# Layer 0's front of a two-layer AdaLN kernel: inverse roots by ln and exp on ScalarE, other orders on the engines, a shorter routing

## The chip, the cores and the metric

The kernel runs on one NeuronCore of a Trainium2 chip. The metric is device time in microseconds (us) of the whole program, one launch; lower is better. Engines: PE is TensorE, DVE is VectorE, ACT is ScalarE, POOL is GpSimd, SP is SyncE, which here only issues DMAs. Each engine works through its own queue in order, and queues wait for each other by semaphores.

## The reference, cut to what matters

A batch of 8 sequences of 512 tokens with 128 channels goes through two layers, each an attention part and a mixture-of-experts part with modulated layernorms. The change is in layer 0, up to the table that says which tokens each expert takes:

```python
mod = (_silu(L0_c) @ L0_wmod).reshape(8, 6, 1, -1); sa, ca, ga, sb, cb, gb = ...
h = _layernorm(x) * (1 + ca) + sa
u = rmsnorm(h) * norm_w                       # x * rsqrt(mean(x*x) + 1e-6)
# a first-order recurrence over the 512 tokens for 64 states, then y = states @ C + D
x = x + ga * y
h = _layernorm(x) * (1 + cb) + sb
wg_n = wg / max(norm(wg), 1e-4)
idx = argmax(softmax((h @ w_red) @ wg_n.T))   # one of 8 experts for each token
# each token goes through its expert only
```

A layernorm needs 1/sqrt(variance + eps) for each token, the rmsnorm 1/sqrt(mean square + eps).

## The kernel before, in words

The 4096 tokens lie as 32 tiles of 128 tokens. A tile holds 64 tokens of each of two sequences (a pair), so there are 4 pairs `bp` of 8 tiles each (1024 columns). Everything in the front is written by hand, pair by pair, as five straight lists of instructions, one for each engine; the order in a list is the order on that engine. Stage `k` is 0 for the first layernorm, 1 for the second.

For each pair: `measure(k, bp)` (DVE: 8 bn_stats, L1088, and five small operations, L1093 to L1097, that give sum and variance); `root` (ACT, sqrt of 8 columns, L741); `rates` (DVE, reciprocal L1102 and a product L1103); the normalising, half a pair on ACT (`norm`, L748) and half on POOL (`norm_too`, L506); `turn_rows` (PE transposes, L1725); for k=0 `first_hT` and `squares` (ACT, L771 and L781), `up_and_squares` (PE, L1735 and L1737: projections and sums of squares), `rms_and_up` (ACT, L788 sqrt and L789 copy), `invert_rms` (DVE reciprocal of 512 columns, L1107), `scale_up` (DVE, L1112), `scan` (DVE, the recurrence, L1118), `read_states` (PE, L1747), `add_y0` (DVE, L1123, which adds the result to x in place and needs POOL's `add_d`, L499, to have been there first). For k=1: `second_hT` (ACT, L795), `first_logits` (PE, 8 products of 8 columns each for a pair, L1764), and `back_rows` (PE, L1757) with `rows_back` (ACT, L803), which turn the rows back so that SP can store them.

After the last logits (semaphore `lg_mm`) DVE does the routing: maximum and one-hot choice (L1210 to L1218), two products on PE that count tokens ahead and in all (L1806, L1807), sums over tiles (L1223 to L1237), slot numbers, one-hot matrices for slots and tiles (L1248 to L1250, L1205), and 32 products on PE (L1820) that give the list of tokens by slot. PE's part of layer 1's modulation (L1717, L1704) lies between the counting and these. `tokens_set` then lets POOL gather rows (L558), and the expert loop follows. From the loop on, the program is the same in both kernels.

Pools and buffers don't decide an order here: each buffer has its place, and the waits are written out. Two pairs share each buffer in turn (`bp % 2`).

## Time and profile before

| | us |
|---|---|
| median of 3 runs | 815.23 (805.23 to 819.42) |
| the profiled execution, its time | 815.39 |
| its span, within that | 813.7 |
| x's first pair measured, start | 8.15 |
| last logits done, routing begins on DVE | 76.15 |
| token list done (end of L1256) | 94.49 |
| first product of the expert loop | 104.80 |

Over the span PE is busy 709.0 us (87%), DVE 640.1 (79%), POOL 579.5 (71%), ACT 476.6 (59%). A span begins with the first instruction and ends with the last; the time of the execution is 1.7 us longer. Line numbers are those of the kernel before. The granted clock is the share of TensorE's full clock: 1.00 is 2.4 GHz, 0.50 is 1.2 GHz. The trace counts an fp32 product as two records.

### The profile page before, as it was taken

The page shows a single profiled execution, that of the slowest core. Times are in us where ns is not written, and L with a number is a line of the kernel's source. Part 1 is how long each engine was busy: PE and PEld are TensorE (multiplying, and loading weights), DVE is VectorE, ACT ScalarE, POOL GpSimd, SP SyncE. Part 2 cuts the span into 40 slices and gives each one's busy share as a digit, 9 for nine tenths or more (in the row PEclk, how much of TensorE's full clock was granted, in tenths as well). Part 3 has the DMA queues.
Part 4 walks back from the last instruction along what each step waited for, and adds up shares of the span by engine and source line. Part 5 has one row for each costly group of instructions (what it writes and reads, how often), then busy time and mean ns, then how long its engine had stood idle before and what let it go on. Part 6 is the DMA issues. An engine that isn't in the chain of part 4 may idle for free.

```text
span 813.7 us, 34138 instructions
## 1 busy us (share of the span) xinstructions
PE 709.0 (87%) x14873; PEld 650.1 (80%) x14874; DVE 640.1 (79%) x1048; ACT 476.6 (59%) x757; POOL 579.5 (71%) x431
## 2 busy tenths in 40 slices
PE   4568778767899999999999999999999998776997
PEld 3357577767788899998899898888999888676897
DVE  6994745379678989999899998999899998866215
ACT  5735234328746756786676677667667764548510
POOL 4811277267789889989889988888788788732750
PEclk8685599999899999999999999999999999985999
DMA  8401324310520000000000000000000000061128
GB/s 336 178 27 53 118 75 96 73 37 9 153 71 13 8 6 6 8 10 6 6 6 8 19 3 3 18 3 3 4 16 4 3 17 17 3 231 56 50 61 293
DMA packets 33583, 42.89 MB, mean 53 GB/s; under 512 B 4000, under 2 KB 25648, under 8 KB 32928
## 3 DMA queue, kind: packets, MB, share of 16 engines
q1 hardware_dynamic: 29856, 33.99, 12.2%
q0 software_dynamic: 3296, 6.76, 3.6%
q8 instruction: 117, 1.92, 1.0%
q14 instruction: 26, 0.21, 0.1%
q10 hardware_dynamic: 288, 0.01, 0.0%
HBM read 26.65 MB, written 14.09 MB: 50 GB/s over the span
## 4 chain that ended last, share of the span: by engine, by line
PE 68%; DVE 12%; issue 10%; POOL 4%; DMA 2%; ACT 2%; DVEq 1%; POOLq 0%; SPq 0%; ACTq 0%
PE psum L1900 18%; PE psum L1955 7%; PE psum L1933 6%; PE psum L2000 6%; PE psum L1991 4%; PE psum L1948 4%; PE psum L1962 4%; PE psum L1970 3%; PE psum L1838 3%; PE psum L1941 2%; PE psum L2258 1%; PE psum L1764 1%; PE psum L1848 1%; DVE small L1430 1%; POOL y_rows L713 1%
## 5 line engine op out<-in xcount | busy, mean ns | idle before, releaser
L1900 PE MATMUL psum<-hT,w_qkv 128*128 128x128 f32 x1408 | 175.7, 282 | 5.8 <-ACT hT L914 2.7
L1900 PEld LDWEIGHTS psum<-hT,w_qkv 128*128 128x128 f32 x1408 | 166.0, 196 | 9.4 <-ACT hT L914 2.8
L617 POOL TENSOR_TENSOR arena<-arena,small 128x1024 f32<-128x1024 f32 x56 | 106.1, 1916 | 40.3 <-DVE small L1449 40.2
L596 POOL TENSOR_TENSOR arena<-arena 128x1024 f32<-128x1024 f32 x56 | 106.8, 1907 | 14.1 <-ACT arena L957 13.1
L582 POOL TENSOR_TENSOR arena<-arena 128x1024 f32<-128x1024 f32 x56 | 106.7, 1905 | 0.1
L1442 DVE TENSOR_REDUCE small<-arena 128x16 f32<-128x1024 f32 x60 | 73.0, 1218 | 12.7 <-ACT arena L946 10.5
L621 POOL TENSOR_TENSOR arena<-arena 128x1024 f32<-128x1024 f32 x28 | 65.9, 2355 | 13.1 <-DVE arena L1469 13.1
L1430 DVE TENSOR_REDUCE small<-psum 128x16 f32<-128x1024 f32 x60 | 72.8, 1215 | 0.2 <-PE psum L2000 0.2
L1436 DVE TENSOR_TENSOR arena<-psum,small 128x1024 f32<-128x1024 f32 x60 | 70.4, 1214 | 0.1
L926 ACT ACTIVATE arena<-psum 128x1024 f32<-128x1024 f32 x28 | 28.7, 1025 | 70.0 <-PE psum L1900 70.0
L558 POOL DMA_INDIRECT arena<-h_rows,route x39 | 39.7, 1018 | 39.2 <-issue 37.7
L2000 PE MATMUL psum<-arena 64*64 64x128 f32 x1792 | 61.0, 277 | 7.4 <-issue 4.4
L1955 PE MATMUL psum<-w_o,arena 128*128 128x128 f32 x512 | 65.5, 282 | 0.9 <-ACT arena L973 0.6
L946 ACT ACTIVATE arena<-arena 128x1024 f32<-128x1024 f32 x60 | 62.9, 1051 | 4.7 <-DVE arena L1436 4.5
L1933 PE MATMUL psum<-arena 64*128 64x64 f32 x1344 | 61.8, 230 | 3.7 <-issue 2.2
L1955 PEld LDWEIGHTS psum<-w_o,arena 128*128 128x128 f32 x512 | 60.5, 194 | 4.8 <-issue 3.4
L2000 PEld LDWEIGHTS psum<-arena 64*64 64x64 f32 x1792 | 51.2, 134 | 11.9 <-issue 10.0
L1933 PEld LDWEIGHTS psum<-arena 64*128 64x128 f32 x1344 | 49.5, 139 | 10.5 <-issue 2.8
L931 ACT ACTIVATE arena<-psum 128x1024 f32<-128x1024 f32 x28 | 28.7, 1026 | 35.2 <-PE psum L1933 35.2
L1461 DVE TENSOR_TENSOR arena<-arena,psum 128x1024 f32<-128x1024 f32 x28 | 34.0, 1216 | 17.5 <-PE psum L1991 17.4
L544 POOL DMA_INDIRECT arena<-o_rows,route x32 | 33.0, 1030 | 20.4 <-DMA o_rows<-arena 13.6
L859 ACT ACTIVATE arena<-psum,route 128x128 f32<-128x128 f32 x78 | 21.4, 380 | 43.8 <-PE psum L1838 43.8
(334 smaller groups left out, 1624.0 us busy)
## 6 DMA issues: line engine op xcount, KB each, us to landing
y_rows<-hT SPq DMA_DIRECT2D x8, 512.0 KB, 6.7
arena<-in_L_W_rows SPq DMA_DIRECT2D x2, 2048.0 KB, 10.6
arena<-y_rows SPq DMA_DIRECT2D x8, 512.0 KB, 8.0
o_rows<-arena SPq DMA_DIRECT2D x9, 256.0 KB
x_sb<-in_x_rows SPq DMA_DIRECT2D x4, 512.0 KB, 6.1
arena<-in_L_W_rows SPq DMA_DIRECT2D x2, 1024.0 KB, 9.7
arena<-in_W_in_rows SPq DMA_DIRECT2D x4, 512.0 KB, 14.9
arena<-in_W_out_rows SPq DMA_DIRECT2D x4, 512.0 KB, 9.4
```

Source lines behind the costliest of these rows:

```text
L582: pool.tensor_tensor(w4, w4, d4.unsqueeze(3).to_broadcast([P, 2, HP, D]), ALU.mult).then_inc(done, 1)
L596: pool.tensor_tensor(x3, x3, lr[:, tile_of(t) * 32 + k * H:tile_of(t) * 32 + k * H + H].unsqueeze(2).to_broadcast([P, H, D]), ALU.mult).th ...
L617: pool.tensor_tensor(z4, z4, r3.unsqueeze(3).to_broadcast([P, 8, 2, CH]), ALU.mult).then_inc(done, 1)
L621: pool.tensor_tensor(g_tok, g_tok, p_tok, ALU.mult).then_inc(g_done, 1)
L946: act.activation(z, z, ACT.Exp, scale=0.5).then_inc(z_exp, 1)
L1430: dve.tensor_reduce(z_max[:, 16 * jh:16 * jh + 16], h3(ps[2 + jh]), AX_X, ALU.max).then_inc(z_maxed, 1)
L1436: dve.tensor_tensor(h3(zs[t % 2][:, jh * 1024:(jh + 1) * 1024]), h3(ps[2 + jh]), z_max[:, 16 * jh:16 * jh + 16].unsqueeze(2).to_broadcast( ...
L1442: dve.tensor_reduce(z_sum[t % 2][:, 16 * jh:16 * jh + 16], h3(zs[t % 2][:, jh * 1024:(jh + 1) * 1024]), AX_X, ALU.add).then_inc(z_added, 1)
L1900: mm = pe.matmul(ps[bank][:, p * P:(p + 1) * P], w_qkv[:, j * HD + p * P:j * HD + (p + 1) * P], hT[:, at:at + P], start=True, stop=True)
L1933: mm = pe.transpose(out[:, col((r, 2), (n, HP))], of[half(r), at(n):at(n) + P], eye[half(r), :])
L1955: mm = pe.matmul(y_bank(t), oT_buffer(t)[:, n * P:(n + 1) * P], w_o[:, n * C:(n + 1) * C], start=(n == 0), stop=(n == HP - 1))
L2000: mm = pe.matmul(out, w_in[t % BP][half(r), col((be, 2), (p, HP))], x4[half(r), :, p, be, :], start=True, stop=True)
```

## The change

1. `root` and `rms_and_up` take ln instead of sqrt, and an exp with scale -0.5 follows on ACT, which gives the inverse root. The reciprocals on DVE (L1102, L1107 and one for the experts' norms) go. For the four pairs the exp of the rmsnorm is a new ACT step, `inverse_rms(bp)`. One table set holds both functions; it is loaded behind the third exp of the start. ACT's list has three table loads up to the expert loop instead of four: the one in front of the exp of the logits goes.
2. Other orders on ACT, DVE, POOL and PE. On DVE `measure(0, 1)` stands ahead of `rates(0, 0)`; on ACT `root(0, 1)` stands ahead of `norm(0, 0)`, and `norm(0, 1)` directly behind it.
3. `keep_warm` products, whose results nobody reads: 10 at the start, 9 behind the gates, 4 ahead of `up_and_squares(0)`, 4 ahead of `first_logits(2)`.
4. Routing: the logits are read from PSUM, the one-hot matrix is written as bf16 at once, eight scans of 32 columns become one of 256, a subtraction goes into the counting matrix (`before_less` holds -1 and 0), tiles are counted by a shift instead of compare and reduce, and the right-hand sides of the 32 products are made in four parts, so that PE may start after the first.

SP's list is the same. The diff, cut to its core:

```diff
+            chain.link(pool.tensor_scalar(before_less, before_less, -1.0, None, ALU.add))
+            chain.link(pool.memset(later_tiles, 1.0))
+            chain.link(pool.memset(later_tiles.rearrange("p (e t) -> p e t", t=T)[:, :, 0], 0.0))
...
             norm_too(0, 0)
+            norm_too(0, 1)
             pool.wait_ge(a0_gates, 2)
             pool.wait_ge(a0_in, 16 * 3)
             chain.link(pool.tensor_tensor(d_gated.rearrange("p (b c) -> p b c", c=C), over_pairs(mod0, 0), over_tiles(d_bc, BP), ALU.mult))
-            norm_too(0, 1)
             add_d(0)
+            add_d(1)
             norm_too(0, 2)
-            add_d(1)
+            add_d(2)
             norm_too(0, 3)
-            add_d(2)
             add_d(3)
...
+            act.preload_act_table_set("natural_log_exp_and_others")
...
                 act.wait_ge(fr_var[k], bp + 1)
-                act.activation(rstd[:, a:b], var[:, a:b], ACT.Sqrt, bias=ln_eps, scale=1.0 / C).then_inc(fr_std[k], 1)
+                chain.link(act.activation(rstd[:, a:b], var[:, a:b], ACT.Ln, bias=ln_eps, scale=1.0 / C))
+                act.activation(rstd[:, a:b], rstd[:, a:b], ACT.Exp, scale=-0.5).then_inc(fr_std[k], 1)
...
                 act.wait_ge(a0_up, bp + 1)
                 after(act, a0_scan, bp - 1)
-                act.activation(rms[bp % 2], ps[2][:, L:2 * L], ACT.Sqrt, bias=rms_eps, scale=1.0 / C).then_inc(a0_rms, 1)
+                act.activation(rms[bp % 2], ps[2][:, L:2 * L], ACT.Ln, bias=rms_eps, scale=1.0 / C).then_inc(a0_rms, 1)
                 act.activation(ups[bp % 2], ps[2][:, 0:L], ACT.Copy).then_inc(a0_rms, 1)
+
+            def inverse_rms(bp):
+                act.wait_ge(a0_rms, 2 * bp + 1)
+                act.activation(rms[bp % 2], rms[bp % 2], ACT.Exp, scale=-0.5).then_inc(a0_rec, 1)
...
             def rates(k, bp):
                 a, b = bp * NC, (bp + 1) * NC
                 dve.wait_ge(fr_std[k], bp + 1)
-                chain.link(dve.reciprocal(rstd[:, a:b], rstd[:, a:b]))
                 dve.scalar_tensor_tensor(sums[:, a:b], sums[:, a:b], -0.5, rstd[:, a:b], ALU.mult, ALU.mult).then_inc(fr_rates[k], 1)
-
-            def invert_rms(bp):
-                dve.wait_ge(a0_rms, 2 * bp + 1)
-                dve.reciprocal(rms[bp % 2], rms[bp % 2]).then_inc(a0_rec, 1)
...
             measure(0, 0)
+            measure(0, 1)
+            rates(0, 0)
             dve.wait_ge(mod_out, 1)
             plus = mod_cols[0].rearrange("c (k s b) -> c k s b", k=2, s=2)[:, :, 0, :]
             dve.tensor_scalar(plus, plus, 1.0, None, ALU.add).then_inc(cols_set, 1)
-            rates(0, 0)
-            measure(0, 1)
+            dve.wait_ge(mod_out, 2)
+            chain.link(dve.tensor_scalar(half_sign, ps[3], 0.0, 0.5, ALU.is_ge, ALU.subtract))
+            rates(0, 1)
+            dve.wait_ge(gw, 32)
+            chain.link(dve.tensor_tensor(wg_n[0:E, :], wg_s[0:E, :], wg_s[0:E, :], ALU.mult))
+            chain.link(dve.tensor_reduce(wg_t[0:E, 0:1], wg_n[0:E, :], AX_X, ALU.add))
...
             chain.link(dve.scalar_tensor_tensor(mod0[:, :], mod0[:, :], 0.5, half_sign, ALU.max, ALU.mult))
-            rates(0, 2)
             dve.sem_inc(a0_gates, 1)
             dve.tensor_tensor(c_gated.rearrange("p (b c) -> p b c", c=C), over_pairs(mod0, 0), over_tiles(cmat, BP), ALU.mult).then_inc(a0_gates, 1)
+            measure(0, 2)
             dve.wait_ge(gw, 34)
-            chain.link(dve.tensor_scalar(wg_t[0:E, 1:2], wg_n[0:E, 0:1], 1e-4, None, ALU.max))
-            chain.link(dve.reciprocal(wg_t[0:E, 2:3], wg_t[0:E, 1:2]))
             dve.tensor_scalar(wg_n[0:E, :], wg_s[0:E, :], wg_t[0:E, 2:3], None, ALU.mult).then_inc(gw, 1)
-            measure(0, 3)
+            rates(0, 2)
             dve.wait_ge(gw, 36)
             dve.tensor_copy(wg_t[0:16, :], ps[3][0:16, 0:E]).then_inc(gw, 1)
-            invert_rms(0)
-            rates(0, 3)
+            measure(0, 3)
+            dve.wait_ge(gw, 38)
+            dve.tensor_copy(w_gate, ps[3][:, 512:512 + E]).then_inc(gw, 1)
             scale_up(0)
             scan(0)
-            dve.wait_ge(gw, 38)
-            dve.tensor_copy(w_gate, ps[3][:, 512:512 + E]).then_inc(gw, 1)
-            invert_rms(1)
+            rates(0, 3)
             add_y0(0)
+            measure(1, 0)
             scale_up(1)
-            measure(1, 0)
             scan(1)
             rates(1, 0)
-            invert_rms(2)
             scale_up(2)
+            scan(2)
             add_y0(1)
-            invert_rms(3)
-            scan(2)
+            measure(1, 1)
             scale_up(3)
             scan(3)
...
-            dve.tensor_copy(logits, ps[2][:, L:L + T * E]).then_inc(lg_out, 1)
-            dve.wait_ge(lg_out, 1)
+            logits = ps[2][:, L:L + T * E]
             chain.link(dve.tensor_reduce(mx, te(logits), AX_X, ALU.max))
             chain.link(dve.tensor_tensor(te(shifted), te(logits), over_e(mx), ALU.subtract))
             chain.link(dve.scalar_tensor_tensor(te(pick), te(shifted), 0.0, over_t(first_w), ALU.is_equal, ALU.mult))
             dve.tensor_reduce(m2, te(pick), AX_X, ALU.max).then_inc(oh_done, 1)
             dve.wait_ge(oh_done, 1)
-            chain.link(dve.tensor_tensor(te(onehot), te(pick), over_e(m2), ALU.is_equal))
-            dve.tensor_copy(onehot_b, onehot).then_inc(rhs_ready, 1)
+            dve.tensor_tensor(te(onehot_b), te(pick), over_e(m2), ALU.is_equal).then_inc(rhs_ready, 1)
...
-            before_p, totals = ps[3][:, 0:256], ps[3][:, 512:768]
-            for e in range(E):
-                last = dve.tensor_tensor_scan(te(cum)[:, :, e], ones_f[:, 0:T], te(totals)[:, :, e], 0.0, ALU.mult, ALU.add)
-            chain.link(last)
-            chain.link(dve.tensor_tensor(rank, cum, totals, ALU.subtract))
-            chain.link(dve.tensor_tensor(rank, rank, before_p, ALU.add))
-
-            cnt = te(cum)[:, T - 1, :]
-            c3 = n_cmp[:, 0:E * T].rearrange("p (e t) -> p e t", t=T)
-            chain.link(dve.tensor_tensor(c3, cnt.unsqueeze(2).to_broadcast([P, E, T]), over_t(edges, E), ALU.is_gt))
-            chain.link(dve.tensor_reduce(n_tiles[:, 0:E], c3, AX_X, ALU.add))
+            by_e = lambda ap: ap.rearrange("p (e t) -> p e t", t=T)
+            not_before, totals = ps[3][:, 0:256], ps[3][:, 512:768]
+            chain.link(dve.tensor_tensor_scan(cum, later_tiles, totals, 0.0, ALU.mult, ALU.add))
+
+            cnt = by_e(cum)[:, :, T - 1]
+            dve.tensor_scalar(tile_i[:, 0:E], cnt, float(P - 1), None, ALU.add).then_inc(tiles_counted, 1)
+            chain.link(dve.tensor_tensor(rank, cum, not_before, ALU.add))
+            dve.wait_ge(tiles_counted, 1)
+            chain.link(dve.tensor_scalar(tile_i[:, 0:E], tile_i[:, 0:E], 7, None, ALU.arith_shift_right))
+            chain.link(dve.tensor_copy(n_tiles[:, 0:E], tile_i[:, 0:E]))
             chain.link(dve.tensor_tensor_scan(t_end[:, 0:E], ones_f[:, 0:E], n_tiles[:, 0:E], 0.0, ALU.mult, ALU.add))
             chain.link(dve.tensor_tensor(t_start[:, 0:E], t_end[:, 0:E], n_tiles[:, 0:E], ALU.subtract))
-            chain.link(dve.tensor_scalar(t_start[:, 0:E], t_start[:, 0:E], float(P), None, ALU.mult))
-            chain.link(dve.tensor_tensor(te(rank), te(rank), over_t(t_start[:, 0:E]), ALU.add))
-            chain.link(dve.tensor_tensor(rank, rank, onehot, ALU.mult))
-            chain.link(dve.tensor_reduce(slot_f, te(rank), AX_X, ALU.add))
+            chain.link(dve.scalar_tensor_tensor(by_e(rank), t_start[:, 0:E].unsqueeze(2).to_broadcast([P, E, T]), float(P), by_e(rank),
+                                                ALU.mult, ALU.add))
+            chain.link(dve.tensor_tensor(by_e(rank), by_e(rank), onehot_b.rearrange("p (t e) -> p e t", e=E), ALU.mult))
+            chain.link(dve.tensor_reduce(slot_f, rank.rearrange("p (e t) -> p t e", t=T), AX_X, ALU.add))
             chain.link(dve.tensor_copy(slot_i[:, 0:T], slot_f))
             chain.link(dve.tensor_scalar(tile_i, slot_i[:, 0:T], 7, None, ALU.arith_shift_right))
+            dve.tensor_copy(tile_b, tile_i)
             chain.link(dve.tensor_copy(tile_f, tile_i))
-            dve.tensor_copy(tile_b, tile_f)
...
             chain.link(dve.tensor_tensor(t4(tile_hot), slot_tiles, over_s(tile_b), ALU.is_equal))
-            dve.tensor_tensor(t4(t_rhs[:, 0:T * 40]), t4(tile_hot), over_s(tile_nb), ALU.mult)
-            dve.tensor_scalar(t_rhs[:, T * 40:T * 80], tile_hot, part_no, None, ALU.mult).then_inc(rhs_ready, 1)
             for i in range(T // 8):
+                here = slice(i * 320, (i + 1) * 320)
+                dve.tensor_tensor(t4(t_rhs[:, 0:T * 40])[:, i], t4(tile_hot)[:, i], over_s(tile_nb)[:, i], ALU.mult)
+                made = dve.tensor_scalar(t_rhs[:, T * 40:T * 80][:, here], tile_hot[:, here], part_no, None, ALU.mult)
+                if i == 0:
+                    made.then_inc(rhs_ready, 1)
                 slots_hot(r_hot, i)
...
+            pe.wait_ge(consts_made, 1)
+            keep_warm(10, ps[2][:, 0:P])
             columns(0)
             gate_rows()
-            pe.wait_ge(consts_made, 1)
+            keep_warm(9, ps[2][:, 0:P])
             turn_rows(0, 0, ps[0])
             pe.wait_ge(mod_out, 1)
-            pe.wait_ge(a0_gates, 1)
-            up_and_squares(0)
             turn_rows(0, 1, ps[1])
             pe.wait_ge(gw, 35)
             pe.transpose(ps[3][0:16, 0:E], wg_n[0:E, :], ident[0:E, 0:E]).then_inc(gw, 1)
-            turn_rows(0, 2, ps[0])
+            keep_warm(4, ps[2][:, 0:P])
+            pe.wait_ge(a0_gates, 1)
+            up_and_squares(0)
             pe.wait_ge(gw, 37)
             pe.matmul(ps[3][:, 512:512 + E], wred_t[0:16, :], wg_t[0:16, :], start=True, stop=True).then_inc(gw, 1)
+            turn_rows(0, 2, ps[0])
             up_and_squares(1)
             pe.wait_ge(gw, 39)
             pe.wait_ge(a0_gates, 3)
             read_states(0)
             turn_rows(0, 3, ps[1])
             up_and_squares(2)
+            read_states(1)
             up_and_squares(3)
             turn_rows(1, 0, ps[0])
-            read_states(1)
+            read_states(2)
             back_rows(0)
+            read_states(3)
+            turn_rows(1, 1, ps[0])
             pe.wait_ge(a0_rms, 8)
             first_logits(0)
-            read_states(2)
-            read_states(3)
-            turn_rows(1, 1, ps[0])
+            back_rows(1)
             first_logits(1)
             turn_rows(1, 2, ps[0])
-            back_rows(1)
             pe.wait_ge(a0_added, 4)
             turn_rows(1, 3, ps[3])
+            keep_warm(4, ps[2][:, 0:P])
             first_logits(2)
             first_logits(3).then_inc(lg_mm, 1)
             back_rows(2)
             back_rows(3)
 
             pe.wait_ge(rhs_ready, 1)
-            pe.matmul(ps[3][:, 0:T * E], before, onehot_b, start=True, stop=True)
-            pe.matmul(ps[3][:, 512:512 + T * E], all_ones, onehot_b, start=True, stop=True).then_inc(cnt_done, 1)
+            hot_by_e = onehot_b.rearrange("p (t e) -> p e t", e=E)
+            by_e = lambda ap: ap.rearrange("p (e t) -> p e t", t=T)
+            pe.matmul(by_e(ps[3][:, 0:T * E]), before_less, hot_by_e, start=True, stop=True)
+            pe.matmul(by_e(ps[3][:, 512:512 + T * E]), all_ones, hot_by_e, start=True, stop=True).then_inc(cnt_done, 1)
```

On DVE, from the last small copy ahead of the first pair's recurrence on. L1107 is the reciprocal of 512 columns, L1112 the scaling, L1118 the scan, L1123 the addition into x. Before:

```order
L1169 COPY arena<-psum 16x8
L1107 RECIPROCAL arena<-arena 128x512
L1102 RECIPROCAL small<-small 128x8
L1103 SCALAR_TENSOR_TENSOR small<-small 128x8
L1112 TENSOR_TENSOR arena<-arena 128x512
L1118 SCALAR_TENSOR_TENSOR arena<-arena 128x512
L1175 COPY arena<-psum 128x8
L1107 RECIPROCAL arena<-arena 128x512
L1123 TENSOR_TENSOR x_sb<-x_sb,psum 128x1024
```

Now, where L1122 is the scaling, L1128 the scan, L1133 the addition:

```order
L1179 COPY arena<-psum 128x8
L1122 TENSOR_TENSOR arena<-arena 128x512
L1128 SCALAR_TENSOR_TENSOR arena<-arena 128x512
L1117 SCALAR_TENSOR_TENSOR small<-small 128x8
L1133 TENSOR_TENSOR x_sb<-x_sb,psum 128x1024
L1103 BN_STATS arena<-x_sb 128x6 x8
```

The two long reciprocals and the wait of the second one are gone from between scan and addition; the third pair's are gone likewise.

On PE, the last third of the front, beginning with the second pair's `read_states`. L1747 is `read_states`, L1757 `back_rows`, L1764 `first_logits`, L1725 `turn_rows`. Before:

```order
L1747 MATMUL psum<-arena 64x128 x16
L1757 MATMUL psum<-ident,hT 128x64 x16
L1764 MATMUL psum<-arena,hT 128x8 x8
L1747 MATMUL psum<-arena 64x128 x32
L1725 MATMUL psum<-ident,arena 128x64 x16
L1764 MATMUL psum<-arena,hT 128x8 x8
L1725 MATMUL psum<-ident,arena 128x64 x16
L1757 MATMUL psum<-ident,hT 128x64 x16
L1725 MATMUL psum<-ident,arena 128x64 x16
L1764 MATMUL psum<-arena,hT 128x8 x16
```

Now, beginning with the third pair's; L1751 is `read_states`, L1761 `back_rows`, L1768 `first_logits`, L1729 `turn_rows`, L1699 the products that nobody reads:

```order
L1751 MATMUL psum<-arena 64x128 x16
L1761 MATMUL psum<-ident,hT 128x64 x16
L1751 MATMUL psum<-arena 64x128 x16
L1729 MATMUL psum<-ident,arena 128x64 x16
L1768 MATMUL psum<-arena,hT 128x8 x8
L1761 MATMUL psum<-ident,hT 128x64 x16
L1768 MATMUL psum<-arena,hT 128x8 x8
L1729 MATMUL psum<-ident,arena 128x64 x32
L1699 MATMUL psum<-ident 128x128 x4
L1768 MATMUL psum<-arena,hT 128x8 x16
```

The first pair's logits (8 products) have moved behind the last `read_states`, and four spare products stand ahead of the last sixteen logits.

On POOL, from the first `norm_too` on; L499 is `add_d`, L513 makes `d_gated`. Before:

```order
L506 TENSOR_SCALAR arena<-x_sb,small 128x128 x4
L513 TENSOR_TENSOR arena<-mod,arena 128x512
L506 TENSOR_SCALAR arena<-x_sb,small 128x128 x4
L499 TENSOR_TENSOR x_sb<-x_sb,arena 128x1024
L506 TENSOR_SCALAR arena<-x_sb,small 128x128 x4
L499 TENSOR_TENSOR x_sb<-x_sb,arena 128x1024
L506 TENSOR_SCALAR arena<-x_sb,small 128x128 x4
L499 TENSOR_TENSOR x_sb<-x_sb,arena 128x1024 x2
L506 TENSOR_SCALAR arena<-x_sb,small 128x128 x16
```

Now, where L508 is `norm_too`, L501 `add_d`, L516 `d_gated`:

```order
L508 TENSOR_SCALAR arena<-x_sb,small 128x128 x8
L516 TENSOR_TENSOR arena<-mod,arena 128x512
L501 TENSOR_TENSOR x_sb<-x_sb,arena 128x1024 x2
L508 TENSOR_SCALAR arena<-x_sb,small 128x128 x4
L501 TENSOR_TENSOR x_sb<-x_sb,arena 128x1024
L508 TENSOR_SCALAR arena<-x_sb,small 128x128 x4
L501 TENSOR_TENSOR x_sb<-x_sb,arena 128x1024
L508 TENSOR_SCALAR arena<-x_sb,small 128x128 x16
```

The second pair's normalising has moved ahead of `d_gated`, and the third pair's behind two of the additions to x.

## Rows read from the trace of the kernel before

**Rows 1.** The page's first line: the profiled execution.
```profile
span 813.7 us, 34138 instructions
```
**Rows 2.** Windows by stage: start:end, length; busy PE, PEld, DVE, ACT, POOL; clock; DMA share; GB/s.
```profile
8.15:33.05 24.90, 14.84 (x88) 9.07 (x88) 23.60 (x78) 18.07 (x37) 14.02 (x21) 0.66 0.86 345
33.05:53.42 20.37, 12.07 (x146) 8.21 (x144) 18.30 (x26) 11.95 (x20) 7.54 (x9) 0.92 0.10 28
53.42:76.15 22.73, 19.23 (x178) 18.16 (x180) 12.15 (x51) 10.74 (x22) 5.25 (x12) 0.65 0.08 24
76.15:94.49 18.34, 14.44 (x82) 9.80 (x82) 13.36 (x42) 8.86 (x13) 0.00 (x0) 0.59 0.28 87
```
**Rows 3.** Groups by line, first 96 us: busy, mean ns, idle before.
```profile
L1107 DVE RECIPROCAL arena<-arena 128x512 f32<-128x512 f32 x4 | 13.4, 3343 | 1.2 <-ACT arena L788 1.2
```
**Rows 4.** Chain of waits, up to the expert loop: start, us, what.
```profile
48.95 3.35 DVE arena L1107
...
69.16 6.96 PE psum L1764 x32
```
**Rows 5.** Timeline of the front: start, us, engine line operation [idle before].
```profile
11.44 1.64 DVE L1088 BATCH_NORM_STATS2 arena<-x_sb 128x6 f32<-128x128 f32 x8
...
15.68 1.45 ACT L781 ACTIVATE arena<-psum,small 128x512 f32<-128x512 f32 x2
...
19.30 0.18 ACT L815 ACTIVATE arena<-arena 8x1 f32<-8x1 f32 x1
...
23.04 0.57 ACT L789 ACTIVATE arena<-psum 128x512 f32<-128x512 f32 x1
...
31.69 1.36 DVE L1118 TENSOR_TENSOR_SCAN arena<-arena 128x512 f32<-128x512 f32 x1
...
41.75 0.30 ACT L741 ACTIVATE small<-small 128x8 f32<-128x8 f32 x1 [1.03 <-DVE small L1097]
```
**Rows 6.** Timeline, VectorE beside GpSimd.
```profile
24.19 2.41 DVE L1094 TENSOR_TENSOR arena<-arena 128x8 f32<-128x8 f32 x1
...
24.22 2.36 POOL L499 TENSOR_TENSOR x_sb<-x_sb,arena 128x1024 f32<-128x1024 f32 x1
...
31.16 3.02 POOL L506 TENSOR_SCALAR arena<-x_sb,small 128x128 f32<-128x128 f32 x4 [0.53 <-DVE small L1103]
```
**Rows 7.** Timeline, TensorE, in order of time.
```profile
45.80 1.96 PE L1747 MATMUL psum<-arena 64*64 64x128 f32 x32
...
48.34 1.95 PE L1764 MATMUL psum<-arena,hT 128*128 128x8 f32 x16
...
53.42 3.68 PE L1747 MATMUL psum<-arena 64*64 64x128 f32 x32 [3.14 <-DVE arena L1118]
...
58.80 1.96 PE L1747 MATMUL psum<-arena 64*64 64x128 f32 x32 [1.70 <-DVE x_sb L1123]
...
96.84 4.60 PE L1695 MATMUL psum<-ident 128*128 128x128 f32 x20 [3.08 <-DVE route L1267]
```
**Rows 8.** Windows of TensorE, 1 us each: busy (count), granted clock, DMA share, GB/s.
```profile
64.00:65.00 1.00, 1.00 (x7) 0.51 0.00 0
```
**Rows 9.** Chain of waits, routing.
```profile
78.37 1.12 PE psum L1757 x16
...
80.07 1.01 DVE arena L1223 x8
...
81.10 0.43 DVE arena L1225
...
82.47 0.43 DVE route L1231
...
86.74 0.83 DVE arena L1249
...
88.03 0.61 DVE arena L1205
...
88.77 5.00 PE psum L1820 x32
```

51 lines of the change are left out of this document (24 added, 27 removed).

## The prediction

> **What bounds the kernel now.** I read the windows by stage first. The front ends where the routing begins, at 76.15 us, the routing takes 18.34 us more, and the rest of the span of 813.7 us [rows 1] is the same program in both kernels. So all that can come or go lies in the first 94.49 us. Up to 53.42 us DVE is busy for 23.60 of 24.90 and 18.30 of 20.37 us, ACT for 18.07 and 11.95, PE for 14.84 and 12.07: DVE is full, the others wait. From 53.42 to 76.15 PE takes over with 19.23 of 22.73 us at a mean granted clock of 0.65 [rows 2]. The groups by line name DVE's largest item, four reciprocals of 512 columns, 3343 ns each, 13.4 us in all [rows 3]. The chain of waits keeps this from being simple: it passes through only one of the four, and then through 6.96 us of logits on PE [rows 4]. The other three ran beside waits of POOL, ACT and PE.
>
> **Up to the first scan.** The first pair starts later now: measure(0,1) costs 1.64 us of bn_stats [rows 5] and about 0.8 of small operations and stands ahead of rates(0,0), and norm(0,0) waits for root(0,1). From DVE's start at 8.15, two measures of 2.4 us give 13.0, the second root and rate 13.5, norm(0,0) and norm(0,1) 16.8, first_hT and squares, 1.45 us each [rows 5], and 0.4 for the two small roots, 20.1. Before, squares(0) ran from 15.68 to 17.13: 3.0 us late. What follows makes it good. On POOL norm_too(0,2) stands behind d_gated and two additions of 2.36 us [rows 6]: about 18.0 + 1.1 + 4.7 = 23.8, plus up to 2.0 where DVE holds it up, so turn_rows(0,2) comes at about 27.5. On ACT, squares(0) at 20.1, root(0,2), first_hT(1), norm(0,2), rms_and_up(0), squares(1) and inverse_rms(0) make 0.5 + 1.45 + 1.65 + 1.25 + 1.45 + 0.6 = 6.9, with 1 to 2 us of waits: 28.5. Scaling and scan (0.7 + 1.36 [rows 5]) would end at 30.6 unhindered; an addition on POOL of 2.36 can stand in front of them: 32.9. I take 31.5, against 33.05: **-1.5 us**, ends -2.5 and 0.
>
> **What the roots cost.** Sqrt of 8 columns was 0.30 us and a small activation without a bias 0.18 [rows 5]; ln then exp is 0.30 + 0.20, in place of 0.30 on ACT and 0.20 of reciprocal on DVE: nothing on the path, 0.2 us off DVE eight times. A 512-column copy took 0.57 us [rows 5]; I take that for the exp, in place of 3.34 on DVE: 2.8 us shorter each time it lies on the path. No trace shows ln; the bounds are the same rows, ±0.1 us each time.
>
> **From the first scan to the last read_states.** Before, this took from 33.05 to 60.76 [rows 7], 27.7 us. Three reciprocals go, 10.0, and 1.2 of waiting for their input [rows 3]. If DVE were the only bound read_states(3) would end at 60.8 - 1.5 - 11.2 = 48.1. It is not: ACT now has, behind inverse_rms(0) at 28.5, root, first_hT, norm, rms_and_up, squares, inverse (6.95 us), then first_hT, root, rms_and_up, inverse, squares, norm, rms_and_up, inverse (8.8), so the last inverse is at 44.3 without a wait and at 46.5 with two or three of a microsecond. Behind it stand scaling, scan, the third pair's addition (1.2) and 1.96 us of products [rows 7]: 46.5 + 0.7 + 1.4 + 1.2 + 2.0 = 51.8. I take **52**, ends 48 and 56: 8.8 us earlier than before.
>
> **PE's tail.** Before, from 60.76 to 76.11 PE did turn, logits(1), turn, back, turn and 16 tiles of logits. Now logits(0), which ran at 48.34 in a gap for 1.95 us [rows 7], lies in the tail, with four spare products. What each costs depends on the clock: 8 tiles of logits took 1.95 us at 2.4 GHz and 6.96 / 2 = 3.48 at 1.2; ten spare products took 4.60 at 1.2 [rows 4, 7], so four take 1.84, and half that at 2.4. The row of the windows at 64 us shows the clock at 0.51 [rows 8], 3.2 us behind the end of read_states(3), with only transposes and logits on PE between, and it stayed at 1.2 GHz through all later transposes and logits. I expect the same: turn 0.7, logits(0) 1.95, back 0.9, logits(1) 3.48, two turns 2.2, spare 1.84, logits(2, 3) 6.96 are 18.0, so 52 + 18.0 = **70.0**, against 76.15: **-6.1 us** for the front (ends -2 and -10). Of the 8.8 us that the head gains the tail gives back 2.7.
>
> **Routing.** Ahead of the counting products, the copy (0.46) and the cast (0.3) go from DVE, which I cost at nothing: these products stand behind back_rows(3) on PE, which ran to 79.49 [rows 9], 0.3 us after DVE had been ready, and that chain stays. Behind them: eight scans 1.01 become one of 256 columns, half of 1.36, say 0.65: -0.4. One subtraction, -0.45. Compare and reduce, 0.43 each, become three operations of 8 columns at 0.2: -0.3. One small product, -0.2, one cast, -0.1. Of the right-hand sides only a quarter stands ahead of PE's start: 0.83 + 0.46 becomes 0.40, -0.9; the four quarters are each shorter (1.0 us with their 0.61 of slots) than the 5.00 / 4 = 1.25 in which PE eats one [rows 9]. Together **-2.4 us**, ends -1.6 and -3.2 (a strided reading of the one-hot matrix by PE and DVE is new; a wider product cost no more than 0.4 here, and I bound it by 0.8). The modulation on PE gets 1.28 us shorter through the missing table load, so it still ends ahead of the slots.
>
> Sum: -6.1 - 2.4 = -8.5, so 815.4 - 8.5 = **807 us**. The profiled execution (815.39) and the median of the runs (815.23) differ by 0.2, so this is also the sum for the median.
>
> **The additions on POOL.** At 24.19 one DVE operation of 8 columns with two SBUF inputs took 2.41 us and ended with POOL's addition of 2.36 that began beside it (26.60 and 26.58) [rows 6]. The reciprocals have one input, and all four took 3.34 [rows 3], though additions ran beside some of them. Four normalisings on POOL took 3.02 us while DVE's scan of 1.36 lay in them [rows 5, 6], so it goes both ways. With the reciprocals gone, measure(0,3), scaling and scan now meet additions. My 31.5 holds one to two of these. The Trainium skill, SBUF — State Buffer, section "Who interferes with whom", says that the two engines take a shared port pair for a whole instruction when the DVE instruction has two SBUF inputs and GpSimd reads SBUF, and that the other blocks fully. The row agrees, once; by the rule all four additions can block, and the sum would be rival C's.
>
> **Rivals.**
> A. *Forecast*, clock falls behind the last read_states: 807, own range 802 to 812. Chance 0.5.
> B. *The clock stays.* The four spare products, denser work ahead of them or a shorter gap keep 2.4 GHz through the tail. Then the tail is 0.7 + 2 + 0.7 + 2 + 1.4 + 0.9 + 3.9 = 11.6, but second_hT(3) on ACT becomes the bound and adds 1 to 2: 52 + 13 = 65, and if it lasts, 1 us of the 5.00 of the token list: 807 - 5 - 1 = 801. For it: dense products bring the clock back, read_states(2) took 3.68 us and read_states(3) 1.96 [rows 7]. Against: ten spare products took 4.60 us, all of it at the pace of 1.2 GHz [rows 7], and here there are four. Chance 0.2.
> C. *POOL's additions block three times more*: 3 x 2.36 = 7.1 on DVE's path: 814. For it: no reciprocal covers them. Against: DVE has slack once ACT is the bound. Chance 0.13.
> D. *Slower: the reciprocals were hidden.* The chain of waits has only one of them, 3.35 us. If no more comes off the path, and the first pair's late start is carried to the end (3.0), and its exp (0.6) and the longer tail (3.48 + 1.84) are paid, the sum is -3.35 + 3.0 + 0.6 + 5.3 - 2.4 = +3.2: 818.5. It decides at the end of read_states(3): past 58 us it is this case. Against: DVE was busy for 0.9 of the time up to there. Chance 0.1.
> That an extra table load spoils the change is excluded: ACT's list has one load for all roots, ahead of the first, which waits for the variance (8.15 + 2.4 = 10.6).
>
> **Numbers.** What is left, 0.07, is scatter: the three runs before reach from -10.0 to +4.2 us around their median. The range of 796 to 816 takes in A, B and C with some of that scatter, and leaves out D and the low end. A measurement of this kernel tells about 2% from no change, 16.3 us, so faster means below 798.9: a third of B and a little scatter, 0.11. Slower means above 831.5: 0.02. Within: 0.87.
>
> **What would show it.** Right: scan(0) ends at 30 to 33 us, read_states(3) at 49 to 55, the last logits at 67 to 73 with a clock of 0.5, token list 15.9 us later. Wrong: squares or rates that wait in ACT's and DVE's lists for POOL and move read_states(3) past 56; logits at 1.0; counting products above 0.8 us; or an expert loop whose 708.9 us change by more than scatter, which I cost at nothing, since its program is the same.

## The result, and the profile after

The changed kernel takes 803.28 us (median of 20 runs, 797.19 to 810.97), the kernel before 810.41 in the same comparison (805.23 to 819.42): a ratio of 0.9907, 95% interval 0.9880 to 0.9933, so 7.1 us less. Its profiled execution has a span of 795.8 us, 17.9 us less than before. 10.7 us of that come from the expert loop onward (104.80 to 813.7 before, 97.55 to 795.8 after), where the program is the same. In the twelve experiments below this stretch took 695.6 to 705.1 us whatever the front, 698.1 in one with the old orders ("roots only"); so the 708.9 us of the kernel before are the long end of the scatter, and the forecast is judged in the front, by waypoints. The changed kernel was profiled a second time (first of the experiments), which shows how far each waypoint holds.

| end of | before | forecast | after | after, second |
|---|---|---|---|---|
| scan(0) | 33.05 | 31.5 | 34.73 | 34.10 |
| read_states(3) | 60.76 | 52.0 | 56.19 | 54.25 |
| last logits | 76.11 | 70.0 | 70.18 | 71.14 |
| token list | 94.49 | 85.9 | 87.20 | 88.19 |

In the kernel before TensorE ended the logits at 76.11, and the routing's first operation on DVE began at 76.15, where its stage is cut.

The page's first line and the windows by stage (start:end, length; busy PE, PEld, DVE, ACT, POOL; clock; DMA share; GB/s), which answer to [rows 1, 2]; line numbers are those of the changed kernel from here on:

```profile
span 795.8 us, 34239 instructions
```
```profile
7.82:34.73 26.91, 16.02 (x111) 11.59 (x113) 20.34 (x72) 17.68 (x39) 16.66 (x24) 0.76 0.82 326
34.73:56.19 21.46, 16.32 (x198) 11.30 (x196) 16.45 (x52) 17.45 (x36) 8.95 (x13) 0.90 0.10 27
56.19:70.18 13.99, 13.99 (x139) 13.67 (x140) 4.13 (x17) 8.83 (x17) 3.50 (x8) 0.74 0.12 35
70.18:87.20 17.02, 13.76 (x82) 9.43 (x82) 12.28 (x38) 7.58 (x12) 0.00 (x0) 0.70 0.33 96
```

DVE is no longer full in the first two stages (20.3 of 26.9 and 16.5 of 21.5 us). The stage up to the first scan got longer all the same, 26.91 us instead of 24.90. The timeline of DVE, ACT and POOL (start, duration, both us; in brackets the idle time before and what ended it) shows why:

```profile
19.77 1.99 DVE L1108 TENSOR_TENSOR small<-arena 128x8 f32<-128x8 f32 x1
...
21.77 2.31 DVE L1110 TENSOR_TENSOR arena<-arena 128x8 f32<-128x8 f32 x1
...
32.78 0.69 DVE L1122 TENSOR_TENSOR arena<-arena 128x512 f32<-128x512 f32 x1 [2.60 <-ACT arena L799]
33.51 1.22 DVE L1128 TENSOR_TENSOR_SCAN arena<-arena 128x512 f32<-128x512 f32 x1
```
```profile
24.51 0.30 ACT L746 ACTIVATE small<-small 128x8 f32<-128x8 f32 x1 [4.92 <-DVE small L1112]
24.84 0.21 ACT L747 ACTIVATE small<-small 128x8 f32<-128x8 f32 x1
...
29.72 0.69 ACT L794 ACTIVATE arena<-psum,small 128x512 f32<-128x512 f32 x1 [1.80 <-PE psum L1741]
32.11 0.64 ACT L799 ACTIVATE arena<-arena 128x512 f32<-128x512 f32 x1
```
```profile
19.39 4.66 POOL L501 TENSOR_TENSOR x_sb<-x_sb,arena 128x1024 f32<-128x1024 f32 x2
```

Two operations of 8 columns in measure(0,2) last as long as POOL's two additions beside them (19.39 to 24.05); others of their kind took 0.17. So the variance of pair 2 is late, ACT stands idle 4.92 us for it, and PE 6.15 us:

```profile
24.67 0.18 PE L1780 MATMUL psum<-ident,arena 8*16 8x8 f32 x1 [6.15 <-DVE arena L1173]
24.77 2.08 PE L1699 MATMUL psum<-ident 128*128 128x128 f32 x8
26.78 1.98 PE L1739 MATMUL psum<-hT,arena 128*64 128x512 f32 x4
...
52.56 3.63 PE L1751 MATMUL psum<-arena 64*64 64x128 f32 x32 [1.49 <-DVE x_sb L1133]
...
59.29 3.46 PE L1768 MATMUL psum<-arena,hT 128*128 128x8 f32 x16
64.58 1.96 PE L1699 MATMUL psum<-ident 128*128 128x128 f32 x8
66.38 3.80 PE L1768 MATMUL psum<-arena,hT 128*128 128x8 f32 x32
...
81.51 4.96 PE L1830 MATMUL psum<-arena 128*128 128x80 bf16 x32 [0.64 <-DVE arena L1209]
```

In PE's list the transpose of the gate's weights (L1780) and four spare products (L1699) stand ahead of up_and_squares(0) (L1739), whose input squares(0) had left on ACT at 19.6. It starts at 26.78, 7 us later. The spare products are 2.0 us of the chain of waits. In the tail the last logits take 3.80 us instead of 6.96 [rows 4]: the clock, which had fallen at 59, comes back. A window of 1 us; the third value from the right is the granted clock, 0.85 here and 1.00 in the next window, and 0.51 in [rows 8]:

```profile
66.00:67.00 1.00, 1.00 (x11) 1.00 (x9) 0.00 (x0) 1.00 (x2) 0.00 (x0) 0.85 0.00 0
```

The routing takes 17.02 us instead of 18.34. The timeline of its DVE part, and the first of PE's two counting products:

```profile
74.59 0.69 DVE L1225 TENSOR_TENSOR_SCAN arena<-arena,psum 128x256 f32<-128x256 f32 x1 [2.03 <-PE psum L1817]
...
77.12 0.62 DVE L1237 TENSOR_TENSOR arena<-arena 128x256 f32<-128x256 f32 x1
77.78 0.60 DVE L1238 TENSOR_REDUCE route<-arena 128x32 f32<-128x256 f32 x1
```
```profile
73.49 0.61 PE L1816 MATMUL psum<-arena,masks 128*128 128x256 bf16 x1
```

The same three in the kernel before:

```profile
84.00 0.42 DVE L1236 TENSOR_TENSOR arena<-arena 128x256 f32<-128x256 f32 x1
84.46 0.42 DVE L1237 TENSOR_REDUCE route<-arena 128x32 f32<-128x256 f32 x1
```
```profile
79.42 0.40 PE L1806 MATMUL psum<-arena,masks 128*128 128x256 bf16 x1
```

The one scan (0.69) is as cheap as forecast. The product with the one-hot matrix and the reduce over it, now read with a stride (and the one-hot matrix as bf16), take 0.62 and 0.60 instead of 0.42 each, and the counting products 0.61 and 0.63 instead of 0.40 and 0.42, all four of them at the low clock.

### The profile page after: what moved, and what is told of

It is laid out like the page before. It is cut to its first block, busy times and chain, and to the rows that moved or that the text cites. A ratio compares the mean times of both kernels' runs of the same rounds, so it can differ in the third digit from the quotient of the medians.

```text
span 795.8 us, 34239 instructions
## 1 busy us (share of the span) xinstructions
PE 707.7 (89%) x14927; PEld 651.7 (82%) x14928; DVE 624.7 (79%) x1031; ACT 478.3 (60%) x769; POOL 581.5 (73%) x433
## 3 DMA queue, kind: packets, MB, share of 16 engines
q1 hardware_dynamic: 29856, 33.99, 12.7%
## 4 chain that ended last, share of the span: by engine, by line
PE 66%; DVE 12%; issue 9%; POOL 5%; DMA 3%; ACT 3%; DVEq 1%; POOLq 0%; SPq 0%; ACTq 0%
PE psum L1910 17%; PE psum L1965 6%; PE psum L1943 6%; PE psum L2010 6%; PE psum L2001 4%; PE psum L1958 3%; PE psum L1972 3%; PE psum L1980 3%; PE psum L1699 2%; PE psum L1951 2%; PE psum L2268 2%; PE psum L2244 2%; PE psum L2233 2%; PE psum L1848 1%; PE psum L1768 1%
## 5 line engine op out<-in xcount | busy, mean ns | idle before, releaser
L1943 PEld LDWEIGHTS psum<-arena 64*128 64x128 f32 x1344 | 49.1, 138 | 13.3 <-issue 4.0
L546 POOL DMA_INDIRECT arena<-o_rows,route x32 | 33.1, 1034 | 20.2 <-DMA o_rows<-arena 13.4
## 6 DMA issues: line engine op xcount, KB each, us to landing
arena<-in_L_W_rows SPq DMA_DIRECT2D x2, 2048.0 KB, 11.2
```

Source lines behind the costliest of these rows:

```text
L1943: mm = pe.transpose(out[:, col((r, 2), (n, HP))], of[half(r), at(n):at(n) + P], eye[half(r), :])
```

## The experiments

Twelve runs. Waypoints are ends, in us, of one profiled execution each; the ratio is to the kernel before, measured beside each, with its 95% interval. The first measure begins at 8.15 in the kernel before, at 8.93 in "routing only" and "orders and routing", at 8.30 in "no additions" and between 7.73 and 8.11 in all others; so a difference of about 1 us between two rows can be the start alone.

| kernel | ratio | scan(0) | read_states(3) | last logits | token list |
|---|---|---|---|---|---|
| before | 1 | 33.05 | 60.76 | 76.11 | 94.49 |
| change | 0.9907 (0.9880, 0.9933) | 34.73 | 56.19 | 70.18 | 87.20 |
| change, second look | 0.9924 (0.9888, 0.9960) | 34.10 | 54.25 | 71.14 | 88.19 |
| roots only | 0.9957 (0.9916, 0.9998) | 31.78 | 58.82 | 74.68 | 93.02 |
| routing only | 1.0004 (0.9973, 1.0034) | 34.24 | 62.04 | 77.41 | 94.80 |
| orders and routing | 1.0085 (1.0049, 1.0122) | 38.53 | 68.90 | 85.81 | 102.85 |
| roots and read order | 0.9934 (0.9894, 0.9974) | 31.95 | 59.22 | 76.86 | 95.25 |
| squares first | 0.9869 (0.9828, 0.9909) | 32.87 | 54.51 | 71.02 | 88.26 |
| norm before additions | 0.9923 (0.9890, 0.9955) | 30.98 | 54.76 | 71.30 | 88.55 |
| both of these | 0.9865 (0.9809, 0.9922) | 28.47 | 54.16 | 68.05 | 85.08 |
| no additions | 0.9866 (0.9825, 0.9908) | 30.45 | 50.45 | 67.27 | 84.28 |
| scan first | 0.9885 (0.9856, 0.9914) | 28.46 | 53.39 | 67.26 | 84.28 |
| no spare | 0.9875 (0.9802, 0.9948) | 34.66 | 56.10 | 72.25 | 89.28 |
| twelve spare | 0.9929 (0.9895, 0.9963) | 34.35 | 55.81 | 71.42 | 88.26 |

**The change, a second look.**

> The changed kernel as it is, looked at a second time, to see how far the waypoints of one execution hold. If the program sets them, the first scan ends within 0.5 us of 34.73, the last read_states within 1 us of 56.19, the logits of the last pairs within 1 us of 70.2 and the token list stands 17.0 us behind these. If the granted clock is what moves them, each product after 40 us may come in 1.96 or in 3.6 us, and the waypoints after it shift by 1.6 us for each one: read_states(3) between 54.5 and 58, logits up to 3 us later where the clock does not come back behind the four spare products.

The waypoints hold to 0.6 us at the first scan, 1.9 at the last read_states and 1.0 at the last logits and the token list, a little more at the first two than the expectation's first case allowed. The clock moves them: up_and_squares(1) took 3.5 us in the first profile and 1.9 in this one. After four spare products the clock did not come back:

```profile
62.45 2.07 PE L1699 MATMUL psum<-ident 128*128 128x128 f32 x8
64.31 6.83 PE L1768 MATMUL psum<-arena,hT 128*128 128x8 f32 x32
...
81.44 1.06 PE L1708 MATMUL psum<-arena 128*128 128x8 f32 x8 [0.69 <-ACT mod L769]
82.48 4.97 PE L1830 MATMUL psum<-arena 128*128 128x80 bf16 x32
```
```profile
64.00:65.00 1.00, 1.00 (x7) 1.00 (x7) 0.00 (x0) 1.00 (x2) 0.00 (x0) 0.50 0.00 0
```

So 3 us of the tail change from one execution to the next. And at the low clock the modulation's last products (L1708, to 82.50) end just as the 32 products start: there they end last, 0.2 us behind DVE's first slots (82.34).

**The parts alone.** Roots only: the kernel before, with ln and exp in place of sqrt and reciprocal, the exp right behind `ups`' copy:

```diff
-                act.activation(rms[bp % 2], ps[2][:, L:2 * L], ACT.Sqrt, bias=rms_eps, scale=1.0 / C).then_inc(a0_rms, 1)
+                act.activation(rms[bp % 2], ps[2][:, L:2 * L], ACT.Ln, bias=rms_eps, scale=1.0 / C).then_inc(a0_rms, 1)
                 act.activation(ups[bp % 2], ps[2][:, 0:L], ACT.Copy).then_inc(a0_rms, 1)
+                act.wait_ge(a0_rms, 2 * bp + 1)
+                act.activation(rms[bp % 2], rms[bp % 2], ACT.Exp, scale=-0.5).then_inc(a0_rec, 1)
```

> The kernel before with part 1 of the change alone: ln and exp for all roots, one table set, the rmsnorm's exp right behind the copy of the same pair on ScalarE; all orders, the routing and the products of the kernel before. If the reciprocals bounded VectorE (the prediction's main step), read_states(3) ends at 52 to 55 us instead of 60.8, the logits at about 69 and the token list at about 87.5: ratio 0.991, so the roots alone would be worth what the whole change is worth. If they were hidden (rival D), only one of them comes off: read_states(3) at 58, token list at about 92, ratio 0.997.

Read_states(3) ends at 58.82, 1.9 us earlier than before (1.6 with the starts taken off), though 13.4 us of reciprocals are gone. That is rival D's case of the two expected (58 and 92), not the prediction's main step (52 to 55). A gain of this size in one profile is no more than the two looks at the changed kernel differ; the ratio of 0.9957 bounds the whole effect at 0.2 to 6.8 us. The time went into a wait; DVE and PE in that kernel:

```profile
40.35 1.22 DVE L1120 TENSOR_TENSOR_SCAN arena<-arena 128x512 f32<-128x512 f32 x1
...
48.34 1.22 DVE L1125 TENSOR_TENSOR x_sb<-x_sb,psum 128x1024 f32<-128x1024 f32 x1 [6.10 <-PE psum L1744]
```
```profile
41.11 1.97 PE L1732 MATMUL psum<-hT,arena 128*64 128x512 f32 x4 [3.17 <-ACT arena L784]
...
45.76 2.53 PE L1744 MATMUL psum<-arena 64*64 64x128 f32 x32
```

The second scan had ended at 41.57, but read_states(1) (L1744) stands in the old order behind up_and_squares(3) and a transpose. The reciprocals had covered this wait.

Orders and routing: the changed kernel with sqrt and DVE's reciprocals back in their places (rates and scale_up).

```diff
             def scale_up(bp):
-                dve.wait_ge(a0_rec, bp + 1)
+                dve.wait_ge(a0_rms, 2 * bp + 1)
+                dve.reciprocal(rms[bp % 2], rms[bp % 2]).then_inc(a0_rec, 1)
+                dve.wait_ge(a0_rec, bp + 1)
```

> The changed kernel with part 1 taken back: sqrt on ScalarE, reciprocals on VectorE (the long one directly ahead of the scaling), all new orders, spare products and the routing kept. If the roots carry the gain, the four long reciprocals (13.4 us) come back mostly on the path: read_states(3) at 63 to 66 us, token list at 94 to 97, ratio 1.00. If the orders carry it, read_states(3) stays below 59 and the ratio is 0.995 or less.

It is 0.9% slower than the kernel before, clear of its interval, and later than the expectation's 63 to 66 and 94 to 97. Its group of reciprocals (first 96 us; busy, mean ns, idle before):

```profile
L1112 DVE RECIPROCAL arena<-arena 128x512 f32<-128x512 f32 x4 | 13.4, 3348 | 0.3 <-ACT arena L792 0.3
```

Between this kernel and the changed one lie 12.7 and 14.7 us at read_states(3). Not all of it is the reciprocals. This kernel is already 2.2 to 2.5 us late when measure(0,2) begins (20.27, against 18.11 and 17.73), since its first inputs landed later and a DVE operation at the start took 1.82 us instead of 0.44 (more on this under "routing only"). That leaves 10.5 to 12.1 us, and the chain of waits passes through three of the four reciprocals (at 44.27, 49.82 and 58.63), 10.1 us. So the exchange of the roots is worth about 2 us in the old order and 10 to 12 in the new one, and orders, spare products and routing without it cost 8.1 (7.4 with the starts taken off).

Routing only: the kernel before with the routing part (and the two masks that POOL makes for it).

> The kernel before with the routing part of the change alone. If the routing's gain is its own, the last logits end at 76.15 +- 1 as before and the token list stands 17.0 us behind them instead of 18.34; in time -1.4 us, no change that a median can tell. If the gain in the changed kernel came from the parts around it (rows_back or the modulation, that end earlier there), it stays at 18.3 here.

From the last logits to the token list it is 17.39 us (17.0 expected), 0.95 less than before; the ratio of 1.0004 cannot show that. PE, then DVE's first part of the slot matrix:

```profile
81.60 5.91 PE L1719 MATMUL psum<-arena 128*128 128x512 f32 x8
88.20 1.06 PE L1706 MATMUL psum<-arena 128*128 128x8 f32 x8 [0.69 <-ACT mod L765]
89.11 4.96 PE L1824 MATMUL psum<-arena 128*128 128x80 bf16 x32
```
```profile
87.90 0.68 DVE L1207 TENSOR_TENSOR arena<-iota_b,rows_b 128x1024 bf16<-128x1024 bf16 x1
```

DVE was ready at 88.58, the modulation kept PE until 89.26: 0.5 us of the gain is held back.

The front of this kernel, whose lists are the old ones, is 0.8 to 1.3 us later than before, from the first measure on. Its first microseconds show why, on DVE and POOL:

```profile
6.58 1.79 DVE L1132 TENSOR_SCALAR arena<-arena 128x512 f32<-128x512 f32 x1
```
```profile
6.14 1.95 POOL L485 IOTA iota_b<- 128x1024 bf16 x1
```

Three small operations that POOL does for the new masks put its iota at 6.14 instead of 4.96. DVE's operation has one SBUF input, and where it met the iota it lasted 1.79 us (1.82 in "orders and routing"); in the nine executions where DVE began it ahead of the iota, at 5.71 to 6.02, it took 0.43 to 0.46. With the iota in its old place DVE met it too, for 0.74 us in the kernel before and 1.45 and 1.30 in the two with the roots alone. So about 1 us at the start hangs on when the first inputs land, in either kernel.

**Roots and read order.** The roots only, and TensorE's read_states earlier, as in the change:

```diff
+            read_states(1)
             up_and_squares(3)
             turn_rows(1, 0, ps[0])
-            read_states(1)
+            read_states(2)
             back_rows(0)
+            read_states(3)
+            turn_rows(1, 1, ps[0])
             pe.wait_ge(a0_rms, 8)
             first_logits(0)
-            read_states(2)
-            read_states(3)
-            turn_rows(1, 1, ps[0])
```

> The roots part on the kernel before, and of the changed orders one thing: TensorE's read_states(1) ahead of up_and_squares(3) and turn_rows(1,0), read_states(2) and (3) ahead of first_logits(0). With the roots alone VectorE stood idle 6.1 us for read_states(1), which TensorE did at 45.76 though its scan had ended at 41.5, and the token list came at 93.0. If this order is what kept the reciprocals' gain from showing, read_states(1) comes near 42, read_states(3) ends at 54 to 55 instead of 58.8, and the token list at 88.5 to 90: some 3 to 4 us less than the roots alone, 802 to 804 us against 809. If the gain was lost elsewhere (in ScalarE's and VectorE's orders), read_states(3) still ends at 57 to 59 and the token list at 92 to 93.

I was wrong here: read_states(3) ends at 59.22 and the token list comes 2.2 us later than with the roots alone. The wait went to the next in line. Read_states(1) did come at 41.78, but read_states(3) waited for add_y0(2) on DVE, and that stood behind scan(3) and measure(1,1) in DVE's old list, though its input was ready at 50.76:

```profile
54.18 1.22 DVE L1125 TENSOR_TENSOR x_sb<-x_sb,psum 128x1024 f32<-128x1024 f32 x1
```
```profile
55.54 3.68 PE L1744 MATMUL psum<-arena 64*64 64x128 f32 x32 [3.46 <-DVE x_sb L1125]
```

And first_logits(0), moved out of a gap into the tail, costs 3.5 us there. The ratio doesn't tell it from the roots alone. TensorE's part of the order without VectorE's showed no gain.

**The head.** Four kernels, each the changed one with an edit. Squares first (it also leaves out the four spare products of the head):

```diff
-            pe.wait_ge(gw, 35)
-            pe.transpose(ps[3][0:16, 0:E], wg_n[0:E, :], ident[0:E, 0:E]).then_inc(gw, 1)
-            keep_warm(4, ps[2][:, 0:P])
             pe.wait_ge(a0_gates, 1)
             up_and_squares(0)
+            pe.wait_ge(gw, 35)
+            pe.transpose(ps[3][0:16, 0:E], wg_n[0:E, :], ident[0:E, 0:E]).then_inc(gw, 1)
```

> The changed kernel with up_and_squares(0) ahead of the transpose of the experts' norms, and without the four spare products there. squares(0) is ready at 19.6 us, but the products waited until 26.8 behind that transpose and the spare products. If that wait is on the path, up_and_squares(0) starts at about 19.7, rms_and_up(0) at 27.9 (then norm(0,2) is what ScalarE does before it) instead of 29.7, scan(0) ends at about 33.0 instead of 34.7 and the token list is 1.8 us earlier, 85.4. If the blocked measure(0,2) holds everything anyway (its variance at 24.5), scan(0) moves by less than 0.5 us.

Norm before additions:

```diff
+            norm_too(0, 2)
             add_d(0)
+            norm_too(0, 3)
             add_d(1)
-            norm_too(0, 2)
             add_d(2)
-            norm_too(0, 3)
             add_d(3)
```

> GpSimd's order alone is changed: norm_too(0,2) ahead of add_d(0), norm_too(0,3) ahead of add_d(1). If additions block VectorE's bn_stats (1.99 and 2.31 us in the changed kernel, where one took about 0.17 to 0.35 before), variance(0,2) ends at about 20.8 instead of 24.5 and the transpose of the gate's weights, which TensorE waits for, comes near 21 instead of 24.67; scan(0) then ends at 31.5 to 32.5 instead of 34.73 and the token list about 2 us earlier, 85. If the additions only move on and block other VectorE work by as much (measure(0,3), scaling and scan), variance(0,2) is early but scan(0) or read_states(3) is not: 56 +- 1 and the token list at 87. If bn_stats is slow for another reason, variance(0,2) stays at 24.5.

Both together:

> Both edits of order together: up_and_squares(0) ahead of the gate's transpose on TensorE, and norm_too(0,2), norm_too(0,3) ahead of the additions on GpSimd. If both delays are on the path, scan(0) ends at about 30 (32.87 with the first edit alone), read_states(3) near 52 to 53 and the token list near 84. If the additions only move on, scan(0) at 32 and the token list at 86 to 88. In time: 0 to 3 us below the changed kernel, which a median can hardly tell.

No additions (all four `add_d` and DVE's wait for them left out; x lacks the D term, so this kernel routes other tokens, and only its front is compared):

> The changed kernel without GpSimd's four additions of the D term (left out, so x lacks it; 4 x 2.33 us off GpSimd). In the changed kernel small VectorE operations with two SBUF inputs lasted 1.99 and 2.31 us instead of 0.17 beside them. If that blocking lies on the path, variance(0,2) ends near 20.5 instead of 24.5, no VectorE operation of 8 columns lasts over 0.5 us, scan(0) ends at 31 (34.1 to 34.7 now), and the token list comes 3 to 4 us earlier than 87.2 to 88.2, at 84. If other waits take its place (read_states on TensorE, first_hT and squares on ScalarE), scan(0) is early and the token list stays within 1.5 us of 87.

Each edit moves scan(0) by what was expected or more (32.87, 30.98, 28.47, 30.45), so both delays are real. But at read_states(3) the three reorderings keep little or nothing of it (54.2 to 54.8, against 54.25 and 56.19), and their token lists miss the hoped-for 85.4, 85 and 84 (88.26, 88.55, 85.08). Only leaving the additions out keeps it: 50.45, and 3.9 us less at the token list than in the second look, where both had the low clock in the tail. In "squares first" the additions block as before (2.34 and 2.20 us) and none blocks later; there up_and_squares(1) took 3.7 us at the low clock (1.9 in the second look), and read_states(0) began at 34.08, hardly earlier than the second look's 34.25. In the other two the additions move on and block elsewhere. DVE and POOL of "norm before additions":

```profile
37.09 2.78 DVE L1108 TENSOR_TENSOR small<-arena 128x8 f32<-128x8 f32 x1
```
```profile
32.85 6.99 POOL L501 TENSOR_TENSOR x_sb<-x_sb,arena 128x1024 f32<-128x1024 f32 x3
```

DVE began this operation at 37.09 and got it done when POOL's third addition ended (39.84). Between 34.15 and 37.06 the same additions had not hindered DVE's add_y0 (one input in PSUM) or its bn_stats (one input). Without additions every operation of that kind took 0.16 to 0.27 up to scan(2). (One expectation calls the blocked operations bn_stats; they are the small ones behind it, and the bn_stats took 1.62 to 1.65 throughout.) The port rule of the Trainium skill (SBUF — State Buffer, "Who interferes with whom"), that a DVE instruction with two SBUF inputs contends with a GpSimd instruction that reads SBUF, holds here for every addition that met one, in all thirteen profiles that have them. The price is not the additions' 9.3 us but what of them meets such operations: 3.7 us at scan(0) and 3.9 at the token list in the change.

**The clock in the tail.** No spare: `keep_warm(4, ...)` ahead of first_logits(2) left out. Twelve spare: 12 in its place.

> The changed kernel without the four spare products ahead of first_logits(2). If these brought the clock back (rival B's mechanism, as the profile after suggests), the 16 tiles of logits take 6.96 us again instead of 3.80 and 1.96 of spare products go: token list at 88.4 instead of 87.2, ratio to before 0.992. If the clock would have come back without them, the logits stay near 3.8 and the token list is at 85.2.

> Twelve spare products ahead of first_logits(2) instead of four. Four took 1.96 to 2.07 us, so at 1.2 GHz in every case, and the logits behind them took 3.8 us in two executions and 6.8 in four. If more products ahead bring the clock back surely, the logits of pairs 2 and 3 take 3.75 us, at a price of up to 4.1 us for eight more products (2.1 where the clock returns within them): no gain, token list at 87 to 90. If the return doesn't hang on what stands there, they take 6.8 us here too, and the token list comes at 91 to 92.

TensorE of the kernel with none, then with twelve:

```profile
65.25 7.00 PE L1768 MATMUL psum<-arena,hT 128*128 128x8 f32 x32 [0.69 <-ACT hT L805]
```
```profile
64.22 3.73 PE L1699 MATMUL psum<-ident 128*128 128x128 f32 x24
67.78 3.64 PE L1768 MATMUL psum<-arena,hT 128*128 128x8 f32 x32
```
```profile
65.00:66.00 1.00, 1.00 (x8) 1.00 (x7) 0.00 (x0) 1.00 (x2) 0.00 (x0) 0.55 0.00 0
66.00:67.00 1.00, 1.00 (x11) 1.00 (x10) 0.00 (x0) 1.00 (x2) 0.00 (x0) 1.00 0.00 0
```

Both came nearly as expected. With none the last logits take 7 us (this kernel, and the kernel before), with twelve 3.6 (one execution). With four they take 3.7 to 3.8 us in three executions (the change, both head edits together, scan first) and 6.83 in five (second look, squares first, norm before additions, no additions, orders and routing). Twelve took 3.73 us; the clock rose 1.7 us into them, as the windows show. From read_states(3) to the last logits that kernel takes 15.6 us, between the second look's 16.9 and the change's 14.0: what they cost and what they save nearly cancel. The ratios don't tell none, four and twelve apart. That spare products can bring the clock back is shown by a close pair: up to the last two turns the kernel with none and the change's first profile agree within 0.1 us at every step (logits(1) from 59.20 and 59.29, 3.46 us in both), and only the one with four got the clock back.

What decides it behind four was not varied on purpose, but the eight profiles differ in one thing ahead of them. Logits(1) took 3.46, 3.29 and 3.27 us in the three where the clock came back, and 3.05, 2.97, 2.78, 2.32 and 2.25 in the five where it did not (1.95 would be all at 2.4 GHz, 3.48 all at 1.2). So the clock came back where it had fallen early in logits(1), and stayed low where it had fallen later. This order was found afterwards and is not tested; by it the return would hang on when the clock fell, which moves from one execution of the same program to the next.

**Scan first.** Both head edits, and further: on DVE scale_up(1), scan(1) ahead of measure(1,0), on ACT root(1,0) behind squares(3), on POOL norm_too(1,0) ahead of the additions of pairs 2 and 3.

```diff
             add_y0(0)
-            measure(1, 0)
             scale_up(1)
             scan(1)
+            measure(1, 0)
             rates(1, 0)
```

> The two edits of order together (up_and_squares(0) first on TensorE, norm_too ahead of the additions), and three more: on VectorE scale_up(1) and scan(1) ahead of measure(1,0), on ScalarE root(1,0) behind squares(3), on GpSimd the additions of pairs 2 and 3 behind norm_too(1,0). In e6 scan(1) began at 38.58 though its input was ready at 33.1; it waited for read_states(0), for measure(1,0) and in it 2.85 us for GpSimd's additions. Expected: scan(0) ends at 28.5, scan(1) at 35 to 36, read_states(3) at 48 to 50 (54.16 in e6), token list at 80 to 82 where the clock comes back ahead of the last logits and 83 to 85 where not: 2 to 4 us below e6, so a median of 792 to 795 against 809 and a ratio of 0.98. If norm(1,0), which now comes later on ScalarE and GpSimd, becomes the bound, read_states(3) is early but first_logits(0) starts late, and the token list stays at 85 to 88.

scan(1) ends at 35.09 as expected, read_states(3) at 53.39, not 48 to 50, and the token list at 84.28, not 80 to 82, though the clock came back. Additions again, DVE in measure(1,1), then a wait of 4.87 us on PE and 3.68 us of read_states at the low clock:

```profile
43.72 2.38 DVE L1109 TENSOR_TENSOR arena<-arena 128x8 f32<-128x8 f32 x1
```
```profile
49.71 3.68 PE L1751 MATMUL psum<-arena 64*64 64x128 f32 x32 [4.87 <-DVE x_sb L1133]
```

It has the earliest token list of all complete kernels, 2.9 us ahead of the change's profile. Its ratio of 0.9885 (0.98 was expected) lies below the change's 0.9907 and 0.9924, as does that of both head edits with 0.9865. But the intervals overlap, and "no spare", whose token list is 2.1 us later than the change's, has 0.9875; so that either beats the change is not shown. Both beat the kernel before.

Not tested alone are the spare products of the start (10 and 9) and the four of the head, whose share in what "squares first" gains is open.

## Why the prediction was right, and where it was not

The forecast of 807 was 8.5 us below its own base; the median fell by 7.1 and the token list came 7.3 and 6.3 us earlier. The measured 803.28 lies 3.7 below 807 because the base, 815.4 from three runs, was 5.0 above the later median of 810.41, less the 1.4 that the gain fell short. Part of the agreement is luck: the terms err both ways.

- **Up to the first scan: wrong, in sign.** Forecast -1.5 us, measured +1.7 and +1.1. The measures, the norm and squares(0) came where I had them (squares(0) ends at 19.59, forecast 20.1). Two things failed. I allowed the additions 2.0 us of delay on POOL's side and one on DVE's late; in fact both first additions fell on measure(0,2), 4.0 us more than its two operations need. And I costed the edit on PE's list at nothing: up_and_squares(0) now stands behind a transpose that waits for DVE behind measure(0,2), and behind four spare products. That wait hung the first pair on the third. "No additions" prices the first at 3.7 us of scan(0) (30.45 against 34.10), "squares first" the second at 1.2 to 1.9.
- **What the roots cost: right.** ln and exp of 8 columns took 0.30 and 0.21, the exp of 512 columns 0.64 (forecast 0.57 within 0.1), no table load beyond the one.
- **First scan to last read_states: right in length, half right in the reason.** Forecast 20.5 us, measured 21.46 and 20.15. That read_states(3) ended at 56.19 and 54.25 instead of 52 is mostly the head's error carried on. I had ACT's last inverse (L799) as the step that everything waits for. It came 14.2 us behind scan(0) (13.3 in the second look), forecast 15.0. But from 43.66 on the chain of waits runs over DVE, busy without a gap until add_y0(2) ends at 52.4: the inverse was there at 48.96, the scaling (L1122) began at 49.36, behind measure(1,1). And read_states(3), which I costed at 1.96, took 3.63 and 3.23 at the low clock. The total came right since a shorter chain on ACT and this longer last step nearly cancel. The last inverse and the scaling, in the first profile:

```profile
48.33 0.63 ACT L799 ACTIVATE arena<-arena 128x512 f32<-128x512 f32 x1
```
```profile
49.36 0.69 DVE L1122 TENSOR_TENSOR arena<-arena 128x512 f32<-128x512 f32 x1
```

- **PE's tail: right in one execution, rival B's in the other.** Forecast 18.0 at the low clock; the second look, with it, had 16.89. In the first the clock came back for the last logits, and the tail took 13.99. There the logits' end at 70.18 met the forecast of 70.0 by luck, two errors that cancel: 4.2 us late at read_states(3), 4.0 us short in the tail.
- **Routing: right in sign, too large.** Forecast -2.4 with ends of -1.6 and -3.2, measured -1.32, -1.29 in the second look and -0.95 alone, all short of the nearer end. The strided readings, for which I allowed up to 0.8 in the range and nothing in the sum, cost 0.4 on DVE and about 0.45 in the counting products; and "still ends ahead of the slots" fails at the low clock, where the modulation ends last.
- **Rival C** had the right mechanism at a smaller size: not three more operations of 2.36 but one more, of 1.99 beside 2.31. **Rival D**'s premise was right for the old order (the roots alone are worth 1.9 us at read_states(3), 1.5 at the token list). It missed that the change brings an order in which three of the four lie on the path. So did I: the forecast of 11.2 us off DVE's path was argued from how full DVE was, not from the order.

## What to carry to other kernels

The worth of an instruction that goes is a property of the order it stands in: here about 2 us in one and 10 to 12 in the other. Reordered lists have to be costed in all engines at once; for each moved step ask what stands behind the wait it brings, on PE also. In these traces a long GpSimd addition cost VectorE time only where it met operations with two SBUF inputs, so moving it mostly moved the stall: ask what it will meet in its new place. A VectorE operation with one input was not safe beside every GpSimd instruction either (the tensor_scalar beside the iota). And one profile does not settle a change of 2 us: compare the start and the clock of each stage first.

## What the hardware showed that I had not expected

- Small VectorE operations with two SBUF inputs waited out a GpSimd addition: 1.99 and 2.31 us beside two additions in a row, 2.34 and 2.20, 2.85; with no addition beside them such operations took 0.16 to 0.28. Between two additions one operation slipped through in 0.16.
- A VectorE tensor_scalar of 512 columns with one SBUF input lasted 1.79 and 1.82 us where it met a GpSimd iota of 1024 columns (1.95 us), which reads nothing, and 0.43 to 0.46 ahead of it.
- After four spare products (1.96 to 2.07 us) the granted clock came back to 1.00 in three executions and stayed at 0.50 in five; the logits(1) ahead had taken 3.27 to 3.46 us in the three, and 2.25 to 3.05 in the five.
- At 1.2 GHz a bf16 TensorE product of 256 columns whose moving operand is read with a stride took 0.61 us, without one 0.40. A VectorE product and reduce over 256 columns 0.62 and 0.60 instead of 0.42.
